# Deformable bottleneck: one of four interpolation products on ScalarE, added to VectorE's tiles in one instruction

## What is computed

```python
# layer 0: bottleneck with a deformable 3x3 convolution
out = relu(bn1(conv1x1(x, w1)))                  # 1024 -> 256 channels
offset = conv3x3(out, w_off) + b_off             # 18 channels: dy, dx of nine taps
# per tap: four corners of the sampled place, weighted
val = g(y0,x0)*wy0*wx0 + g(y0,x1)*wy0*wx1 + g(y1,x0)*wy1*wx0 + g(y1,x1)*wy1*wx1
out = relu(bn2(einsum('nckhw,ock->nohw', val, w2)))
x = relu(bn3(conv1x1(out, w3)) + x)
# layer 1: masked grouped convolutions (4 groups)
out = relu(gconv1x1(x * mask)); out = relu(gconv3x3(out * mask)) * mask
x = relu(gconv1x1(out) + x)
```

## Time and profile before

| | |
|---|---|
| median of three executions | 2953.07 us (2951.67 to 2953.92) |
| the profiled execution's span | 2953.8 us |
| PE busy | 2809.9 us, 95% |
| DVE busy | 2306.2 us, 78% |
| ACT busy | 1265.0 us, 43% |
| POOL busy | 1246.2 us, 42% |
| mean granted PE clock | 0.984 |

### The profile page before, as it was taken

One profiled execution on the slowest core, in us unless ns is written; L12 is line 12 of the kernel. 1 busy time (PEld: TensorE's weight loads), 2 busy tenths in 40 slices (PEclk: granted clock), 3 DMA queues, 4 the chain that ended last, 5 costly groups with the idle time before them and its releaser, 6 DMA issues.

```text
span 2953.8 us, 45116 instructions
## 1 busy us (share of the span) xinstructions
PE 2809.9 (95%) x12064; PEld 1553.2 (53%) x12064; DVE 2306.2 (78%) x5439; ACT 1265.0 (43%) x2530; POOL 1246.2 (42%) x1160
## 2 busy tenths in 40 slices
PE   7969999999999999999999999999999999999998
PEld 3435555555555555455455555555555555555552
DVE  2138888887878878788787878878888898888871
ACT  1224444444444444444444444444444444444442
POOL 2025544434434434344443434444444455555530
PEclk9989999999999999999999999999999999999999
DMA  7679988888888888888888888888888888888862
GB/s 272 201 251 338 318 285 323 319 318 284 302 294 280 322 299 300 288 277 311 297 326 275 301 294 290 313 300 302 310 293 285 288 329 314 319 311 318 325 240 79
DMA packets 263070, 863.50 MB, mean 292 GB/s; under 512 B 31746, under 2 KB 72834, under 8 KB 254336
## 3 DMA queue, kind: packets, MB, share of 16 engines
q0 software_dynamic: 165888, 604.05, 58.1%
q1 hardware_dynamic: 78592, 190.68, 18.9%
q10 hardware_dynamic: 18432, 67.12, 5.6%
HBM read 747.72 MB, written 114.02 MB: 292 GB/s over the span
## 4 chain that ended last, share of the span: by engine, by line
PE 82%; DVE 9%; issue 5%; ACT 1%; DMA 1%; another core or an unknown queue 1%; POOL 1%; DVEq 0%; SPq 0%; ACTq 0%; POOLq 0%
PE psA L413 11%; PE psR L521 11%; PE psD L501 9%; PE psD L503 9%; PE psD L502 9%; PE psR L553 8%; PE psV L482 8%; PE psA L449 4%; DVE val L952 4%; PE psR L534 4%; PE psR L570 4%; PE psR L576 2%; DVE y L935 2%; PE psD L449 1%
## 5 line engine op out<-in xcount | busy, mean ns | idle before, releaser
L378 POOL DMA_INDIRECT corners<-corner_tables,samples_in x1152 | 1230.8, 1068 | 1607.8 <-DVE val L952 1154.1
L952 DVE SCALAR_TENSOR_TENSOR val<-corners,samples_in,val 128x256 f32<-128x256 f32 x3456 | 1417.3, 478 | 77.8 <-ACT val L698 64.3
L712 ACT ACTIVATE valT_hi<-psV 128x512 fp32r<-128x512 f32 x576 | 311.7, 592 | 898.0 <-PE psD L503 694.5
L962 DVE TENSOR_TENSOR valT_lo<-psV,valT_hi 128x512 fp32r<-128x512 f32 x576 | 370.5, 685 | 264.2 <-ACT valT_hi L712 227.3
L521 PE MATMUL psR<-deformed,w_sb 128*128 128x512 f32 x1024 | 485.5, 616 | 46.8 <-DVE y L883 44.7
L698 ACT ACTIVATE val<-corners,samples_in 128x256 f32<-128x256 f32 x1152 | 490.5, 503 | 33.1 <-DMA corners<-corner_tables,samples_in 25.6
L501 PE MATMUL psD<-valT_hi,w_hi 128*128 128x512 f32 x1152 | 484.4, 421 | 0.4 <-DVE valT_lo L962 0.4
L502 PE MATMUL psD<-valT_hi,w_lo 128*128 128x512 f32 x1152 | 456.3, 396 | 0.0
L503 PE MATMUL psD<-valT_lo,w_hi 128*128 128x512 f32 x1152 | 455.9, 396 | 0.0
L482 PEld LDWEIGHTS psV<-const_sb,val 128*128 128x128 f32 x2304 | 264.5, 142 | 192.7 <-issue 131.1
L413 PE MATMUL psA<-x_sb,w_sb 128*128 128x512 f32 x768 | 356.5, 603 | 5.1 <-DMA x_sb<-in_x 5.1
(11 more groups left out here) (78 smaller groups left out, 1571.5 us busy)
## 6 DMA issues: line engine op xcount, KB each, us to landing
y<-in_x SPq DMA_DIRECT2D x128, 512.0 KB
out<-y ACTq DMA_DIRECT2D x128, 512.0 KB
x_sb<-in_x SPq DMA_DIRECT2D x48, 1024.0 KB
corner_tables<-x_sb SPq DMA_DIRECT2D x128, 256.0 KB
corners<-corner_tables,samples_in POOLq DMA_INDIRECT x1152
y<-in_x SPq DMA_DIRECT2D x8, 2048.0 KB, 10.2
corner_tables<-corners SPq DMA_DIRECT2D x8, 1139.0 KB, 5.7
samples_dram<-samples SPq DMA_DIRECT2D x32, 90.0 KB
```

The costliest lines, as they stand in the source:

```text
L378: nc.gpsimd.indirect_dma_start(corners[:, slot, :], None, table, bass.IndirectOffsetOnAxis(ap=index[:, TAPS * t + k:TAPS * t + k + 1], axi ...
L712: nc.scalar.activation(valT_hi[:, m, :], psV[m][:], ACT.Copy).then_inc(valT_ready, 1)
L952: nc.vector.scalar_tensor_tensor(acc, corners[:, n % GS, corner * CMID:(corner + 1) * CMID], samples_in[:, bpar, w:w + 1], acc, ALU.mult, ...
L962: nc.vector.tensor_tensor(valT_lo[:, m, :], psV[m][:], valT_hi[:, m, :].bitcast(F32), ALU.subtract).then_inc(valT_rest, 1)
```

## The change

ScalarE multiplies corner 3 of each of the tap's four tiles by its weight, in place in `corners`, before it writes the four first corners. VectorE's new `add_products` then adds the four scaled corners to the four tiles of `val` in one instruction of 128x1024, where four multiply-adds (corner 1) began before; it waits until all eight of ScalarE's instructions for the tap are done. Corners 1 and 2 follow as multiply-adds in the places of corners 2 and 3. A tap counts 9 in `fma` (FMA_TAP) instead of 12, and the waits of GpSimd, TensorE and VectorE on `fma` are rewritten to that. GpSimd's slot is free after the last multiply-add of a tile, as before.

```diff
--- before.py
+++ after.py
@@ -33,7 +33,8 @@
 LAG_T, LAG_B, LAG_C, LAG_E = 1, BPI, BPI + 1, BPI + 2
 
 
-N_FMA = TAPS * TILES * 3
+FMA_TAP = 2 * TILES + 1
+N_FMA = TAPS * FMA_TAP
 N_HALO = 2
 N_D = 6
 D_MASKED = 4
@@ -373,7 +374,7 @@
                         if low > LAG_B or TILES * k + t >= GS:
 
                             last = TILES * k + t - GS
-                            pool.wait_ge(fma, N_FMA * h + 12 * (last // TILES) + 9 + last % TILES)
+                            pool.wait_ge(fma, N_FMA * h + FMA_TAP * (last // TILES) + TILES + 2 + last % TILES)
                             pool.sem_inc(pool_waits, 1)
                         nc.gpsimd.indirect_dma_start(
                             corners[:, slot, :], None, table,
@@ -471,7 +472,7 @@
 
                     if "B" not in on:
                         return
-                    pe.wait_ge(fma, N_FMA * h + 12 * (k + 1))
+                    pe.wait_ge(fma, N_FMA * h + FMA_TAP * (k + 1))
                     if low == LAG_B and k == 0:
                         pe.wait_ge(pixels_ready, 2 * LAG_B)
                         pe.wait_ge(coord, N_CRD * (LAG_B - 2) + CRD_PSUM_READ)
@@ -689,11 +690,17 @@
                         act.wait_ge(weights_split, N_SPLIT)
                     if k == 0:
                         act.wait_ge(samples_loaded[bpar], 16 * (block // 2 + 1))
+                    for tile in range(TILES):
+                        n = TILES * (TAPS * bpar + k) + tile
+                        act.wait_ge(gathered[n % GS], 16 * (n // GS + 1) + 16 * (2 * TILES * TAPS // GS) * (block // 2))
+                        w = (3 * TILES + tile) * TAPS + k
+                        last = corners[:, n % GS, 3 * CMID:]
+                        nc.scalar.activation(last, last, ACT.Copy, scale=samples_in[:, bpar, w:w + 1]
+                                             ).then_inc(first_corner, 1)
                     if not fresh:
                         act.wait_ge(val_turned, 2 * (TAPS * block + k - 1))
                     for tile in range(TILES):
                         n = TILES * (TAPS * bpar + k) + tile
-                        act.wait_ge(gathered[n % GS], 16 * (n // GS + 1) + 16 * (2 * TILES * TAPS // GS) * (block // 2))
                         w = TAPS * tile + k
                         nc.scalar.activation(val[:, (bpar + k) % 2, tile, :], corners[:, n % GS, 0:CMID],
                                              ACT.Copy, scale=samples_in[:, bpar, w:w + 1]
@@ -935,6 +942,18 @@
                     nc.vector.tensor_tensor(y[:, par, m, :], psR[m % 2][:], y[:, par, m, :], ALU.add
                                             ).then_inc(out_sum, 1)
 
+                def add_products(k):
+
+                    if ("B" if k < TAPS else "next B") not in on:
+                        return
+                    block, bpar = (h, par) if k < TAPS else (h + 1, odd)
+                    k %= TAPS
+                    slot = TILES * (TAPS * bpar + k) % GS
+                    acc = val[:, (bpar + k) % 2]
+                    dve.wait_ge(first_corner, 2 * TILES * (TAPS * block + k + 1))
+                    nc.vector.tensor_tensor(acc, acc, corners[:, slot:slot + TILES, 3 * CMID:], ALU.add
+                                            ).then_inc(fma, 1)
+
                 def interpolate(k, corner):
 
                     if ("B" if k < TAPS else "next B") not in on:
@@ -945,10 +964,7 @@
                         n = TILES * (TAPS * bpar + k) + tile
                         w = corner * TILES * TAPS + TAPS * tile + k
                         acc = val[:, (bpar + k) % 2, tile, :]
-                        if corner == 1:
-                            dve.wait_ge(first_corner, TILES * TAPS * block + TILES * k + tile + 1)
-                        else:
-                            dve.wait_ge(fma, N_FMA * block + 12 * k + 4 * (corner - 2) + tile + 1)
+                        dve.wait_ge(fma, N_FMA * block + FMA_TAP * k + 1 + (tile + 1 if corner == 2 else 0))
                         nc.vector.scalar_tensor_tensor(acc, corners[:, n % GS, corner * CMID:(corner + 1) * CMID],
                                                        samples_in[:, bpar, w:w + 1], acc, ALU.mult, ALU.add
                                                        ).then_inc(fma, 1)
@@ -969,7 +985,8 @@
 
 
                 beside = {k: each(valT_low, *([k - 1] if k else [])) for k in range(TAPS)}
-                c1, c2, c3 = ({k: [corner(k + 1, c)] for k in range(TAPS)} for c in (1, 2, 3))
+                c1 = {k: [lambda k=k: add_products(k + 1)] for k in range(TAPS)}
+                c2, c3 = ({k: [corner(k + 1, c)] for k in range(TAPS)} for c in (1, 2))
                 if "A" in on:
                     beside[0] += c1[0] + each(y_add, 0) + c2[0] + [mask_expand] + each(y_add, 1) + c3[0]
                 else:
@@ -994,7 +1011,8 @@
                     beside[7] += c1[7] + c2[7] + c3[7] + [positions]
                     beside[8] += c1[8] + c2[8] + each(valT_low, 8) + c3[8] + [coordinates]
                 if low == LAG_B:
-                    for c in range(1, 4):
+                    add_products(0)
+                    for c in (1, 2):
                         interpolate(0, c)
                 for k in range(TAPS):
                     for f in beside[k]:
```

## The result

| | before | after |
|---|---|---|
| median of the runs | 2953.16 us | 3053.68 us (3051.19 to 3058.93) |
| ratio, 95% interval | | 1.0345 [1.0333, 1.0357] |
| profiled span | 2953.8 us | 3053.6 us |
| mean granted PE clock | 0.984 | 0.987 |

The account below looks back on a forecast made before the run. TensorE was taken to set the pace, VectorE mattering only where TensorE waits for it. Block losses of 40, 46 and 8 us gave +94 on 2953, so 3047 us; range 3000 to 3097 (70%), 3000 to 3105 with rivals 2 and 3.

Parts of the forecast that it names:

- the 350 to 450: Before the new addition: VectorE's total idle time put down to ScalarE, in us, against 64.3 before.
- The steady block: Blocks with all stages (steps 10 to 31): late additions make PE wait, 1.8 us a block, +40 us over 22.
- The gain at the block's start: At conv3(3), which waits for y_add(1): VectorE's shorter tap gets there earlier, gaining 0.36 us a block.
- The end block: Blocks without conv1 (steps 32 to 39): less PE work beside each tap, 5.7 us lost a block, +46 over eight.
- the 2.4: End block's later places, gconv3(0), turn_val(3) and conv3(0): 2.4 us lost together, an estimate.
- The first two blocks: Steps 8 and 9, not walked: loss between the two other kinds, 1.8 to 5.7 us each, +8 us.
- rival 2: At PE's waits: they take TensorE's clock down, 1.5 us more a block, 45 in all, 3092 us; chance 8%.
- Rival 1: At conv3(6): ScalarE's batch is in time and VectorE's relief decides, faster, 2942 us; chance 5%.
- Rival 3: At y_add(0): later out stores delay the residual's load, up to 35 us more, 3082 us; chance 12%.
- Rival 4: Whole kernel: waits absorbed just as far as the gain reaches, 2953 us within 6; chance 5%.

Follow-up runs that it names:

- after_flat: The changed kernel with every loop written out, nothing else changed; 2992.59 us, ratio 1.0138 to the kernel before.
- before_flat: The kernel before with every loop written out, nothing else changed; 2894.22 us, ratio 0.9804 to the kernel before.
- e_load: The kernel before plus the change's four scalings on ScalarE; VectorE keeps twelve multiply-adds, third group with factor 1, starting tile by tile; 2988.01 us.
- e_last_flat: The changed kernel with first corners ahead of scalings, the addition last and every loop written out; 2881.39 us, ratio 0.9763 to the kernel before.
- e_last: The changed kernel with first corners written ahead of the scalings, VectorE's multiply-adds first and the addition last; loops kept; 2956.13 us.

## Why the prediction came out as it did

The time lies 7 us over the 3047 forecast, and the mechanism named in it is the one that the runs show.

**Prices.** The addition measured 1223 ns (1.22 taken, bounds 1.05 to 1.58), a scaling 503 ns, ScalarE's busy time 1717.7 us (1726). VectorE's wait for ScalarE came to 445.7 us, at the upper end of the 350 to 450. (In the range, one and a half times the sum gives 3094, not 3097; nothing hangs on it.)

**The steady block.** after_flat and before_flat can be laid over each other from a block's first valT_low (at 1045.25 and 1069.16). PE's timeline, before_flat: conv3(2) and conv3(3) in one row, turn_val(1), conv3(6) and conv3(7) in one row, then gconv3(0) and turn_val(8):

```profile
1041.96 3.83 PE L521 MATMUL psR<-deformed,w_sb 128*128 128x512 f32 x8
1046.08 1.16 PE L482 MATMUL psV<-const_sb,val 128*128 128x128 f32 x8 [0.29 <-DVE valT_lo L962]
...
1068.41 3.60 PE L521 MATMUL psR<-deformed,w_sb 128*128 128x512 f32 x8
...
1104.23 1.13 PE L570 MATMUL psR<-gb,gw_sb 64*128 64x512 f32 x4
...
1106.26 1.04 PE L482 MATMUL psV<-const_sb,val 128*128 128x128 f32 x8
```

and after_flat:

```profile
1066.31 3.60 PE L522 MATMUL psR<-deformed,w_sb 128*128 128x512 f32 x8
1069.99 1.16 PE L483 MATMUL psV<-const_sb,val 128*128 128x128 f32 x8
...
1092.74 1.98 PE L522 MATMUL psR<-deformed,w_sb 128*128 128x512 f32 x4 [0.26 <-DVE y L890]
1094.99 1.98 PE L522 MATMUL psR<-deformed,w_sb 128*128 128x512 f32 x4 [0.26 <-DVE y L890]
...
1130.02 1.13 PE L571 MATMUL psR<-gb,gw_sb 64*128 64x512 f32 x4 [0.76 <-DVE gb L934]
...
1132.30 1.16 PE L483 MATMUL psV<-const_sb,val 128*128 128x128 f32 x8
```

With 23.91 taken off, conv3(6) starts 0.42 late, gconv3(0) 1.88, turn_val(8) 2.13, and so on:

| place | forecast | measured |
|---|---|---|
| conv3(6) | +0.5 | +0.42 |
| conv3(7) | +0.5 | +0.63 |
| gconv3(0) | +0.8 | +0.83 |
| turn_val(8) and its tap | +0.35 | +0.38 |
| the block's start | -0.36 | -0.46 |
| sum | +1.8 | +1.80 |

Over 22 blocks: 40 us, the forecast's term. Between the two profiles with loops (after and before) these blocks came to 38.

The gain at the block's start has the forecast's size partly by luck. It was taken from conv3(3)'s wait for y_add(1), 0.28 us in one block of before. Without loops that place gives 0.23 (the eight matmuls of conv3(2) and (3) last 3.83 in before_flat, 3.60 in after_flat), and another 0.22 comes from turn_val(1)'s wait for valT_low(0), which the prediction did not name.

**The end block** (step 37; from 2606.93 and 2688.75). before_flat, conv3(4) to (7) and the next group; then after_flat, the same, with turn_val(3) and gconv3(0):

```profile
2613.31 3.66 PE L521 MATMUL psR<-deformed,w_sb 128*128 128x512 f32 x8
...
2620.48 3.60 PE L521 MATMUL psR<-deformed,w_sb 128*128 128x512 f32 x8
...
2629.54 3.65 PE L534 MATMUL psR<-y,gw_sb 128*64 128x512 f32 x16 [1.78 <-ACT y L731]
```

```profile
2697.02 1.98 PE L522 MATMUL psR<-deformed,w_sb 128*128 128x512 f32 x4 [1.72 <-DVE y L890]
2699.26 1.98 PE L522 MATMUL psR<-deformed,w_sb 128*128 128x512 f32 x4 [0.26 <-DVE y L890]
...
2705.14 1.98 PE L522 MATMUL psR<-deformed,w_sb 128*128 128x512 f32 x4 [0.22 <-DVE y L890]
2707.38 1.98 PE L522 MATMUL psR<-deformed,w_sb 128*128 128x512 f32 x4 [0.26 <-DVE y L890]
2709.65 1.16 PE L483 MATMUL psV<-const_sb,val 128*128 128x128 f32 x8 [0.29 <-DVE valT_lo L978]
...
2739.68 0.70 PE L571 MATMUL psR<-gb,gw_sb 64*128 64x512 f32 x2 [1.10 <-DVE gb L934]
```

conv3(4) to (7) lose 1.89, 0.57, 0.38 and 0.63 (forecast 1.7, 0.5, 0.6, 0.5); turn_val(3) 0.57, gconv3(0) 1.18 and the next conv3(0) 0.62, together 2.37 against the 2.4 that I had only estimated. So the 2.4 holds, though one of its three causes was wrong: conv3(0) waits for out_relu's last tile (L747), not for deformed_relu. Sum 5.84 (5.7).

**The first two blocks** lost 1.35 and 4.82, with the profile's start 1.2 us later: 7.4, forecast 8. They had not been walked, so the agreement is luck, and 1.5 of step 9's loss is of another kind (below).

**What was mis-sized** is the term of eight like end blocks: 54 us between the two profiles where the forecast had 46. Three of them (steps 32, 35 and 36) lost 8.8, 8.5 and 7.7, some 8 us together over the others, which is about the error of the forecast. Steps 35 and 36 lie at the second loop's turn (above). Step 32 is the last with the offsets' copy (L677), 1.8 us that ScalarE does ahead of the scalings; its addition stood 4.2 us, and in after_flat PE stood 2.92 before gconv3(0):

```profile
2344.22 2.08 PE L571 MATMUL psR<-gb,gw_sb 64*128 64x512 f32 x4 [2.92 <-DVE gb L934]
2346.23 2.68 PE L577 MATMUL psR<-y,const_sb 128*128 128x512 f32 x4
```

```profile
2343.00:2349.00 6.00, 4.78 (x12) 1.93 (x13) 5.96 (x12) 3.24 (x9) 3.24 (x2) 0.72 0.28 89
```

The granted clock of these 6 us is 0.72 in the mean, so a part of them stood at the lower of its two levels (1.2 and 2.4 GHz), and the matmuls behind the wait take 2.08 and 2.68 instead of 1.13 and 1.98: 1.65 us more. That is **rival 2**. It shows in two more blocks of after, where before stays at full clock: in step 9, where a turn_val behind valT_low takes 1.94 us (1.16 in before),

```profile
337.95 1.94 PE L483 MATMUL psV<-const_sb,val 128*128 128x128 f32 x8 [2.13 <-DVE valT_lo L978]
```

```profile
337.00:343.00 6.00, 5.05 (x20) 4.43 (x21) 4.21 (x8) 3.12 (x8) 4.27 (x4) 0.72 0.65 193
```

which costs 1.5 us, and twice in step 36, behind the second loop's turn (3.0 and 1.5 us). Together with step 32 that is 7.6 us: rival 2 came true in three blocks, not in all. The mean clock did not fall.

**What the waits view hides.** I expected PE's waits for VectorE to grow by 90 us; they grew by 63 (27.9 at y_add, 28.8 at gb_mask, 5.9 at valT_low). Another 31 are in PE's busy time, 2809.9 before and 2841.2 after with the same matmuls, and some 6 in waits for ScalarE and others. Without loops, at the same mean clock (0.993 and 0.992), the busy time grows by 27 (2793.1 to 2819.8). The rows above show how: eight matmuls without a wait occupy 3.60 us; cut by waits, twice four occupy 1.98 each, 0.36 more. A wait shown as 0.26 cost 0.42 and 0.63.

**The other rivals.** Rival 1's point of decision was a delay of 1.58 us at conv3(6): e_load's 1.6 us left the steady blocks unmoved, after's 2.1 to 2.4 cost 1.8. Rival 3: in after the loads of y take a median of 7.1 us from issue to landing, under its 7.5,

```profile
y<-in_x SPq DMA_DIRECT2D x128, 512.0 KB, 7.1
```

and VectorE shows no wait for them. Rival 4 is out by the measured time.

The Trainium skill ("VectorE: DVE Perf Modes", "Rules for kernel authors") asks for few chained VectorE instructions. Here the runs both disagree and agree with it: nine instead of twelve lost 100 us while the first of the nine waited for a batch, and won 12.8 us (e_last_flat against before_flat) once it came last.

## What to carry to other kernels

One instruction in place of several also joins their waits: it starts with the last producer, and everything behind it in its queue waits too, so count the producer's pitch times the batch against the slack of what stands behind it. Put the wide instruction where its inputs are long done, at the end of the chain, or make the inputs in time in which the producer idles. And when a saving on a side engine brings nothing, look at the loops' turns too, not at the body alone.

## What the runs showed that I had not expected

- A turn of the loop over steps 12 to 29 costs 7.0 us in before: VectorE starts nothing for 6.0 us, and the granted clock of the next 6 us is 0.67. ScalarE's own gap is 5.9 to 7.2 us in after and 6.4 to 7.5 in e_last; in before its branch is over in 0.3. Written out, the kernel before is 58 us faster (0.9804), more than the change won in any order. That the gap comes with the loop's turn is shown by its absence in the written-out kernels. That the engine waits for its instructions there is read from the packets in the gap and not tested by itself, and so is the part of ScalarE's 72 more instructions.
- A wait of 2.92 us on PE was followed by 6 us at a granted clock of 0.72. After a wait of 1.78 us in step 37 of after_flat the stretch of 2714 to 2720 shows 1.00, but after one of 1.86 in step 36 of after the stretch of 2695 to 2701 shows 0.72: the length of the one wait does not decide it.
- Of 117 us less work on VectorE (2307.3 in before_flat, 2190.0 in e_last_flat), an engine that was 80% busy, 12.8 reached the end, and these only without the loops.
